# A graph network of four layers: SyncE copies some of the rows that GpSimd gathers, in two of five passes

## The reference

```python
# third layer (P2): attention of 4 heads
e = e_src[src] + e_dst[dst]; e = where(e >= 0, e, 0.2 * e)
exp_e = exp(e - max(segment_max(e, dst), 0)[dst])
alpha = exp_e / (segment_sum(exp_e, dst)[dst] + 1e-10)
out = segment_sum(alpha[..., None] * h[src], dst)
# fourth layer (P3)
agg = segment_sum(edge_weight[:, None] * x[src], dst)
out = leaky_relu((agg + x) @ W1.T + b1 + agg * x @ W2.T + b2, 0.2)
```

## Time and profile before

| | us |
|---|---|
| median of 3 runs | 11406.7 (11404.31 to 11411.17) |
| the profiled execution | 11410.4, its span 11408.5 |
| busy: GpSimd | 8190.2 (72%), 8632 instructions |
| busy: VectorE | 7216.0 (63%) |
| busy: ScalarE | 5413.3 (47%) |
| busy: TensorE | 956.1 (8%) |
| P2, 7187 to 9207 us: GpSimd, VectorE, ScalarE busy; DMA share | 1520.0, 991.9, 765.7; 0.38 |
| P3, 9313 to 11311 us: the same | 1510.5, 741.8, 629.7; 0.33 |

### The profile page before, as it was taken

How to read it: one execution, slowest core, us unless ns; L and a number is a source line. 1 busy time by engine, 2 the same in 40 slices (tenths; PEclk the granted TensorE clock), 3 DMA queues, 4 the chain that set the end, 5 groups by cost and what they waited for, 6 DMA issues and landing times.

```text
span 11408.5 us, 38369 instructions
## 1 busy us (share of the span) xinstructions
PE 956.1 (8%) x3312; PEld 677.7 (6%) x3312; DVE 7216.0 (63%) x6971; ACT 5413.3 (47%) x6326; POOL 8190.2 (72%) x8632
## 2 busy tenths in 40 slices
PE   4122222221000000030000001100000000000001
PEld 3111111110000000010000000000000000000001
DVE  8845555553888888869999997454444543333334
ACT  6244444442666666546766765333333333333332
POOL 2177777777777777667777776777777767777776
PEclk8555565555555555565555555555555555555555
DMA  8756666663666666546666665333333333333333
GB/s 307 275 193 204 202 206 200 204 202 109 215 211 216 210 216 211 198 148 224 223 222 226 220 226 160 96 110 113 110 113 111 112 96 103 107 103 106 106 104 97
DMA packets 792030, 1943.01 MB, mean 170 GB/s; under 512 B 214034, under 2 KB 425962, under 8 KB 791369
## 3 DMA queue, kind: packets, MB, share of 16 engines
q1 hardware_dynamic: 459776, 1126.04, 28.0%
q0 software_dynamic: 331904, 814.65, 24.9%
q10 hardware_dynamic: 144, 0.41, 0.0%
HBM read 1201.70 MB, written 738.73 MB: 170 GB/s over the span
## 4 chain that ended last, share of the span: by engine, by line
POOL 61%; issue 24%; DVE 7%; DMA 4%; ACT 2%; PE 1%; POOLq 0%; SPq 0%; DVEq 0%; ACTq 0%
POOL region L1382 58%; DMA region<-x,ix_s 2%; DVE psR L1513 2%; POOL work L1808 1%; DVE region L656 1%; DVE region L657 1%; DVE psB L1430 1%; DVE work L1528 1%; DVE psR L1521 0%; ACT work L1622 0%; POOL start_rows_by_dst L1136 0%; POOL start_ed L972 0%; DMA region<-h,ix_s 0%; POOL start_rows_by_src L1131 0%; PE psR L759 0%
## 5 line engine op out<-in xcount | busy, mean ns | idle before, releaser
L1528 DVE TENSOR_TENSOR_SCAN work<-work,psR 128x1792 f32<-128x1792 f32 (+2 forms) x496 | 1971.3, 3974 | 92.5 <-DVE ix_s L1449 56.5
L1382 POOL DMA_INDIRECT region<-x,ix_s x1612 | 1521.2, 944 | 502.3 <-issue 460.7
L1382 POOL DMA_INDIRECT region<-qm,ix_s x1612 | 1524.0, 945 | 492.6 <-issue 490.1
L1382 POOL DMA_INDIRECT region<-kv,ix_s x1612 | 1524.1, 945 | 491.0 <-issue 484.3
L1382 POOL DMA_INDIRECT region<-k,ix_s x1612 | 1521.5, 944 | 491.2 <-issue 490.9
L1382 POOL DMA_INDIRECT region<-h,ix_s x1612 | 1521.4, 944 | 491.2 <-issue 488.8
L1546 ACT COPY work<-region 128x1664 f32<-128x1664 f32 (+1 forms) x496 | 1162.2, 2343 | 1307.2 <-DMA region<-start_rows_by_dst 775.4
L1430 DVE TENSOR_TENSOR_SCAN psB<-psB,work 128x1792 f32<-128x1792 f32 (+1 forms) x496 | 1485.1, 2994 | 397.8 <-ACT psB L1559 350.8
L1622 ACT COPY work<-work 128x1664 f32<-128x1664 f32 (+2 forms) x496 | 1539.2, 3103 | 0.0
L1621 ACT COPY psR<-work 128x128 f32<-128x128 f32 (+2 forms) x496 | 189.3, 382 | 2463.9 <-DVEq L1529 2463.9
L1458 DVE TENSOR_TENSOR work<-region,psB 128x1664 f32<-128x1664 f32 x372 | 702.1, 1887 | 808.9 <-DMA region<-k,ix_s 528.2
(11 more groups left out here) (339 smaller groups left out, 5050.9 us busy)
## 6 DMA issues: line engine op xcount, KB each, us to landing
region<-start_rows_by_dst SPq DMA_DIRECT2D x248, 832.0 KB, 6.8
state_p<-work SPq DMA_DIRECT2D x124, 936.0 KB, 4.9
state_p<-work SPq DMA_DIRECT2D x124, 884.0 KB, 3.8
region<-start_rows_by_src SPq DMA_DIRECT2D x124, 832.0 KB, 9.9
start_rows_by_dst<-zero_t SPq DMA_DIRECT2D x62, 1664.0 KB, 7.7
state_pA<-work SPq DMA_DIRECT2D x124, 832.0 KB, 4.9
state_p<-work SPq DMA_DIRECT2D x124, 832.0 KB, 3.5
start_rows_by_src<-zero_t SPq DMA_DIRECT2D x1, 59904.0 KB, 163.6
```

The costliest lines, as they stand in the source:

```text
L1382: g_.indirect_dma_start(to[b][:, k, 0:wd_s], None, q.tabs, bass.IndirectOffsetOnAxis(ap=ix_s[b][:, k:k + 1], axis=0))\
L1528: c.do(nc.vector.tensor_tensor_scan(q.st[:, 0:F * (K + 1)], decay_at(q, b)[:, 0:F * (K + 1)], summed[:, 0:F * (K + 1)], 0.0, ALU.mult, ALU ...
```

## The change

It touches P2 and P3. One column in every eight halves, the last one of the second half of pairs 5, 9, 13, ... 61, is no longer gathered by GpSimd: 15 columns a pass, 30 in all. SyncE brings them in two steps. During the four pairs before, it reads that column's 128 row numbers from HBM into registers, 32 at the head of each pair (`numbers_of`), and issues for each number a DMA that copies one row of the table to a buffer in HBM (`row_ahead`), 16 ahead of the near load and the store of each half. Then, in the pair that uses it, it copies the whole column with one DMA to the row buffer (`column_in_sp`), and VectorE waits for that too. The table of row numbers is made once: VectorE copies each such column of `oth_i`, TensorE turns it, ScalarE copies it to SBUF as integers (all between PB and PA), and SyncE stores it to HBM at P2's start. SyncE also waits at the start of P2 and P3 until the tables are complete. GpSimd's loop in these passes has two pairs ahead of it and then a body of four pairs, 15 times. The semaphores that count gathered columns are shared by passes three apart.

The diff without its declarations of four small tensors and two buffers in HBM:

```diff
--- before.py
+++ after.py
@@ -297,6 +300,12 @@
         psrow_src = [stat[:, :, :, :].rearrange("p j a h -> p (j a h)")[:, b * K * 12:(b + 1) * K * 12] for b in range(2)]
+        PAIRS_AHEAD = 4
+        COLS_AHEAD = (IT // 2 - 2) // PAIRS_AHEAD
+        FIRST_AHEAD = PAIRS_AHEAD + 1
+        COL_AHEAD = FIRST_AHEAD * 2 * K + 2 * K - 1
+        assert 2 + PAIRS_AHEAD * COLS_AHEAD == IT // 2
         keys_dram = dram("keys_in", [2, P, C])
         sorted_dram = dram("keys_sorted", [2, P * C])
         pay_dram = dram("payload", [EP, PW])
@@ -334,6 +345,15 @@
             def own(self, what):
                 return S(f"{self.name}_{what}")
+            def gathers(self, b):
+                return K * (IT // 2) - (COLS_AHEAD if self.ahead and b else 0)
+            def rows(self, b, value):
+                i = passes.index(self)
+                return S(f"rows{b}_{i % 3}"), value + sum(16 * q.gathers(b) for q in passes[i % 3:i:3])
             def total(self, what):
                 half = IT // 2
@@ -361,7 +381,10 @@
         P2 = Pass("p2", H2, 32, True, h2_t, ed2_t, edx_t, 136)
         P3 = Pass("p3", 1, D, False, x3_t, None, None, D)
         passes = [PB, PA, P1, P2, P3]
+        AHEAD = [P2, P3]
         for q in passes:
+            q.ahead = q in AHEAD
+            q.ahead_before = AHEAD.index(q) if q.ahead else 0
             q.bv, q.abig, q.st, q.psrow, q.zt, q.prod = bv, abig, st, psrow, zt, prod
             q.early = q in (P1, P2)
             q.dwide, q.wwide = (zt[:, 0:1024], prod_flat[:, 0:1024]) if q.early else (work[:, 0:1024], work[:, 1024:2048])
@@ -1372,15 +1395,38 @@
                 g_.wait_ge(S(nm[0]), nm[1])
             if q.near is not None:
                 g_.indirect_dma_start(head[:, 0:q.HF], None, q.tabd, bass.IndirectOffsetOnAxis(ap=head_i[q.o][:, 0:1], axis=0)).then_inc(q.s("head_in"), 16)
-            with g_.Fori(0, IT // 2) as i:
+            def pair(i, short):
                 for b in range(2):
                     g_.wait_ge(*q.on(f"free{b}", i + 1))
                     if q is P1:
                         g_.wait_ge(q.own(f"next{b}"), i + 1)
                     g_.sem_inc(S("pool_go"), 1)
-                    for k in range(K):
+                    for k in range(K - (short and b)):
                         g_.indirect_dma_start(to[b][:, k, 0:wd_s], None, q.tabs, bass.IndirectOffsetOnAxis(ap=ix_s[b][:, k:k + 1], axis=0))\
-                          .then_inc(q.own(f"rows{b}"), 16)
+                          .then_inc(q.rows(b, 0)[0], 16)
+            if q.ahead:
+                pair(0, False)
+                pair(1, False)
+                with g_.Fori(0, COLS_AHEAD) as j:
+                    for u in range(PAIRS_AHEAD):
+                        pair(j * PAIRS_AHEAD + (u + 2), u == PAIRS_AHEAD - 1)
+            else:
+                with g_.Fori(0, IT // 2) as i:
+                    pair(i, False)
+        def columns_ahead(i):
+            return max(0, (i - 1) // PAIRS_AHEAD)
+        def brought(q, i, b):
+            return q.ahead and b and i >= FIRST_AHEAD and (i - FIRST_AHEAD) % PAIRS_AHEAD == 0
+        def gathered(q, i, b):
+            return 16 * (K * (i + 1) - (columns_ahead(i) if q.ahead and b else 0))
         def heads(t, q):
             return t[:, 0:q.H, :]
@@ -1450,7 +1496,9 @@
                     c.wait()
                     v.sem_inc(q.s(f"free{b}"), 1)
-                v.wait_ge(q.own(f"rows{b}"), i * (16 * K) + 16 * K)
+                v.wait_ge(*q.rows(b, gathered(q, i, b)))
+                if brought(q, i, b):
+                    v.wait_ge(S("column_in"), 16 * (column_number(q, columns_ahead(i) - 1) + 1))
                 if q.near is not None:
                     v.wait_ge(*q.on("held", n + 1))
@@ -1659,6 +1707,50 @@
             sp.dma_start(rows_d[b][:, :, :].rearrange("p t w -> p (t w)")[:, 0:K * q.HF],
                          q.near[0:EP, :].rearrange("(p t) w -> p (t w)", t=T)[:, bass.ds(i * (2 * K * q.HF) + b * K * q.HF, K * q.HF)]).then_inc(q.s(f"near_in{b}"), 16)
+        def numbers_dve(v):
+            nc.vector.tensor_copy(numbers_f[:, :], oth_i[1][:, COL_AHEAD:T:2 * K * PAIRS_AHEAD]).then_inc(S("numbers"), 1)
+        def numbers_pe(pe):
+            pe.wait_ge(S("numbers"), 1)
+            nc.tensor.transpose(numbers_ps[0:COLS_AHEAD, :], numbers_f[:, :], ident[:, :]).then_inc(S("numbers"), 1)
+        def numbers_act(act):
+            act.wait_ge(S("numbers"), 2)
+            nc.scalar.copy(numbers_i[:, :], numbers_ps[0:COLS_AHEAD, :]).then_inc(S("numbers"), 1)
+        def numbers_sp(sp):
+            sp.wait_ge(S("numbers"), 3)
+            sp.dma_start(numbers_t, numbers_i[:, :]).then_inc(S("numbers"), 16)
+            sp.wait_ge(S("numbers"), 19)
+        def column_number(q, j):
+            return q.ahead_before * COLS_AHEAD + j
+        def row_ahead(sp, q, j, r, number):
+            wd = q.tabs.shape[1]
+            sp.dma_start(ahead_t[j, r:r + 1, 0:wd], q.tabs[bass.ds(number, 1), :]).then_inc(S(f"row_ahead{column_number(q, j) % 2}"), 16)
+        def numbers_of(sp, j, a, z):
+            return nc.values_load_multi_w_load_instructions(numbers_t[j:j + 1, a:z], engines=(mybir.EngineType.SP,), min_val=0, max_val=PADN,
+                                                            skip_runtime_bounds_check_because="a row number is the number of a node, at most PADN")[1]
+        def column_in_sp(sp, q, j):
+            wd = q.tabs.shape[1]
+            c = column_number(q, j)
+            sp.wait_ge(S(f"row_ahead{c % 2}"), (c // 2 + 1) * 16 * P)
+            sp.wait_ge(*q.on("free1", FIRST_AHEAD + j * PAIRS_AHEAD + 1))
+            sp.dma_start(gathered_rows(q)[1][:, K - 1, 0:wd], ahead_t[j, :, 0:wd]).then_inc(S("column_in"), 16)
+        def part_of(i):
+            u = i % PAIRS_AHEAD
+            return P * u // PAIRS_AHEAD, P * (u + 1) // PAIRS_AHEAD
         def pass_sp(sp, q):
             for b in range(2):
                 sp.sem_inc(q.s(f"sent{b}"), 16)
@@ -1671,10 +1763,27 @@
                 if q is P1:
                     bias_load(sp, 0, b)
+            if q is AHEAD[0]:
+                numbers_sp(sp)
+            if q.ahead:
+                for nm in q.needs:
+                    sp.wait_ge(S(nm[0]), nm[1])
             def two(i, last):
                 if q is PB:
                     zeros_chunk_sp(sp, i)
+                j = i // PAIRS_AHEAD
+                fetch = q.ahead and j < COLS_AHEAD
+                if fetch:
+                    a, z = part_of(i)
+                    numbers = numbers_of(sp, j, a, z)
                 for b in range(2):
+                    if brought(q, i, 1) and not b:
+                        column_in_sp(sp, q, columns_ahead(i) - 1)
+                    if fetch:
+                        mid = (a + z) // 2
+                        for r in (range(a, mid), range(mid, z))[b]:
+                            row_ahead(sp, q, j, r, numbers[r - a])
                     if not last and q.near is not None:
                         sp.wait_ge(*q.on("made", i * 6 + (3 * b + 1)))
                         near_load(sp, q, i + 1, b)
@@ -2191,6 +2300,7 @@
             with v.If(unsorted(v) < 1):
                 nc.vector.memset(ew[PAD_ROW:P, PAD_COL:T], 0.0).then_inc(S("ew_padded"), 1)
             v.sem_inc(S("edges_ready"), 1)
+            numbers_dve(v)
             pass_dve(v, PA)
             carry_dve(v, PA)
             end0_dve(v)
@@ -2221,6 +2331,7 @@
             src_act(act)
             pass_act(act, PB)
             carry_act(act, PB)
+            numbers_act(act)
             pass_act(act, PA)
             carry_act(act, PA)
             end0_act(act)
@@ -2247,6 +2358,7 @@
             src_pe(pe)
             payload_pe(pe)
             carry_pe(pe, PB)
+            numbers_pe(pe)
             carry_pe(pe, PA)
             end0_pe(pe)
             carry_pe(pe, P1)
```

More of the change, by code:

```diff
@@ L165, in graph_layers_kernel @@
         head = sb("head", [P, D])
+        numbers_f = sb("numbers_f", [P, (IT // 2 - 2) // 4])
+        numbers_i = sb("numbers_i", [(IT // 2 - 2) // 4, P], I32)
+        numbers_ps = psB[:, 3, 256:256 + P]
         bias2 = [sb(f"bias2_{o}", [P, P]) for o in range(2)]
@@ L311, in graph_layers_kernel @@
         x3_t = dram("x3", [NN * P, D])
+        numbers_t = dram("numbers_ahead", [COLS_AHEAD, P], I32)
+        ahead_t = dram("rows_ahead", [COLS_AHEAD, P, 264])
         keyrow_t = [dram(f"keyrow{o}", [P, T], I16) for o in range(2)]
```

## The result

The changed kernel takes 12258.3 us (median of 4 runs, 12253.09 to 12264.41) where the kernel before takes 11408.8 us: 849.5 us more, ratio 1.0745, 95% interval 1.0727 to 1.0764. The time that was predicted was 11535 us, with a range of 11365 to 11850.

A forecast was written before the change was run, and what follows sets the result against it. GpSimd's gathers were taken to bound P2 and P3. From the profiled 11410.4 us, 147 lost in P2 through SyncE's ring and 18.7 gained in P3 gave 11538.7, less 3.7: 11535 us, range 11365 to 11850.

The forecast's parts named there:

- The ring: P2: SyncE's store, rows, near load, its landing, ScalarE's copies, next store; a pair 34.8 us against 32.46.
- the read: SyncE reading 32 row numbers into registers at the head of each pair: 8.0 us, ends 0.9 and 15.4.
- the price of a row copy: SyncE's issue of one row with its address: 0.41 us, ends 0.37 and 0.49; 6.6 us for 16 rows.
- fifth rival: HBM to HBM row copies complete slowly, the column arrives late, VectorE then GpSimd wait: 11520 us, chance 0.02.
- the landing: Time for P2's near load to arrive once issued: 2.5 us, low end 1.9, high end 3.6.
- the address operation: SyncE's multiplication of a row number into an address: 0.12 us, between 0.08 and 0.20.
- rival 1: P2's ring stays under GpSimd's pace, so the spared gathers all count: 11369 us, chance 0.36.
- corner with all terms high: P2's pair with every piece at its high end: 47.0 us, 12265 us in total, called unlikely.
- third rival: P2's ring turns slower, reads over 12 us a pair: 11770 to 12265 us, 0.09 of the main case's chance.
- The far branch: GpSimd's longer loop body makes each turn a far branch of 3.67 us: 11473 us if P2 holds, chance 0.03.
- the late column: Same as the fifth rival: row copies land too slowly and VectorE waits for the column; 11520 us, chance 0.02.
- The turn of the loop: A branch back in GpSimd's loop: 0.045 us.

The follow-up runs named there:

- e8: Changed kernel with SyncE issuing the near load first in each half, ahead of reads and row copies; 11588.3 us, ratio 1.0157.
- e5: Changed kernel with rows copied to one of two column buffers in SBUF instead of HBM, order on SyncE unchanged; 11370.3 us, ratio 0.9967.
- e6: Changed kernel with both the near load first in each half and rows copied to SBUF; 11367.1 us, ratio 0.9965.
- e18: e6 with PA added, a column in every six halves, and 32 numbers read each half from an aligned place; 11438.9 us, ratio 1.0027.
- e17: e6 with the row numbers stored one element (4 B) further on in HBM; 14047 us on a slower chip, ratio 1.0987.
- e14: e6 with PA added and a column in every six halves, reading 21 or 22 numbers each half; 12296.2 us, ratio 1.0779.
- e16: Same kernel as e18 (e14 with aligned reads of 32 numbers), on a slower chip; 14476 us, ratio 1.132.

## Why the prediction was wrong

**Right: what bounds the kernel, and P3.** A gather is worth 1.248 us while GpSimd is the slowest, and P3 gave 18.8 us against 18.7 forecast.

**Right: the mechanism in P2.** The ring was named piece by piece, and the profile shows each: ScalarE's wait for `region<-start_ed` (16 us a half), GpSimd's for VectorE, the half with the read 3.6 us longer than the other. e8 breaks it and 670 us come back; e5 shortens it and the loss is gone.

**Wrong: the price of a row copy, the term that decides.** It was taken at 0.41 us (ends 0.37 and 0.49) and is 0.925. Its row was that of DMAs of one row with their source in SBUF. The step took over their 0.29 us for a copy from HBM to HBM, although the prediction itself remarks under its fifth rival that the trace has no such row. There the doubt was put into the landing, where it costs nothing, and not into the issue. The ends were set round the address operation (0.08 or 0.20, measured together 0.20 with the gaps) and not round the copy, which was bounded on neither side. e5 is the control: with one side in SBUF a row costs 0.43 to 0.44, even so from 0.228 for the copy and 0.20 for the address where 0.29 and 0.12 had been added up.

**Wrong in the other direction: the read.** 8.0 us were taken for 32 numbers, the range being 0.9 to 15.4, and 3.73 were measured. The argument was a price for each register from a single read of 0.287 us. The Trainium skill ("Runtime: NRT & Kernel Launch", section "Instruction fetch mechanics") gives some 0.2 us for each register even in bulk; for 32 that would be 6.4, an estimate from that page. The traces have 0.12 from an aligned start in P2 and P3, 0.21 in PA and 0.40 from an unaligned one, so the page's figure lies between what one and the same instruction does here, and the measurement decides.

**The landing** was taken at 2.5 us and is 2.3 (before 3.6). That the store ahead of it is gone by then, as argued, e5 and e6 bear out: 1.8 us with rows between store and near load, 3.9 with the near load right behind the store.

With the measured terms the sum is 2 x (0.36 + 14.8 + 2.3 + 0.28 + 3.68) + 3.73 = 46.6 us a pair, against 47.55 in the pair shown, and against 46.9 as the mean of the 60 pairs with rows, which is the 867 us. Of the 11.8 us over the forecast 34.8 the rows are 32 x 0.515 = 16.5, and the read takes 4.3 back and the landing 0.4.

**Luck: that it became slower.** With the measured read and landing and the prediction's own 0.41 a row a pair is 2 x (0.36 + 6.56 + 2.3 + 0.28 + 3.68) + 3.73 = 30.1 us, under 32.46: rival 1's 11369, as e5 then showed. The forecast had the right sign only because the read had been taken at more than twice its price. The prediction's corner with all terms high came to 12265 us, near the result, but by a read of 15.4 us and rows of 0.49: the same sum from wrong terms. The range of 11365 to 11850 left that corner out as unlikely, and a bound for a copy whose kind the trace never shows should have kept it in.

**The rivals.** That the ring stays hidden (0.36) was false for this kernel and true for e5. The measured time lies in the third rival's 11770 to 12265, but not by its condition, reads over 12 us. The far branch (0.03) and the late column (0.02) did not show: the gap between P3's gathers is still 0.30 us, and the column's load landed in 1.8 us at the median. The turn of the loop was given as 0.045 us, where the rows have 0.053 at the median; nothing hangs on it.

## What to carry to other kernels

Before an engine with idle time is given work, write down the order of its operations and look for a load behind that work on which the next store depends: a ring's length counts, not the engine's load. Price an operation only from a row with the same two ends; a DMA from HBM to HBM is no DMA with a side in SBUF. Where the trace has no such row, carry the doubt through to the range. And an engine that issues many small DMAs can become the bound by itself (35.7 us a pair in e8, 16.8 us a half in e18), even in a good order.

## What the runs showed of the hardware

- SyncE's issue of a one-row copy with a register address, median: 0.228 us from HBM to SBUF (512, 528 and 1056 B alike), 0.556 from HBM to HBM in one piece (508 or 524 B), 0.729 in 12 pieces of 44 B, 0.492 in 16 pieces of 32 B.
- A read of 32 neighbouring 4 B numbers from HBM into registers, median: 3.5 to 3.9 us from a multiple of 128 B in P2 and P3, 6.8 in PA, where the DMA share is 0.64 against 0.40 in P2 (e18; that this is the cause is not shown), and 12.9 us with the start 4 B further on (e17). 21 or 22 numbers, mostly from uneven starts: 9.1 us (e14).
- The same program differs by 12% between chips (11407 and 12780 us), and kernels with many small operations on SyncE by up to 27% (e16 14476 us, e18 11439). The cause is open.
